# A four-block network on one core: the first attention's probabilities transposed by the DMA engines in its first half

## What is computed

```
x = x + tanh(g_xattn[1]) * _L1_xattn_ref(_layernorm(x), ctx_1024, Wq, Wk, Wv, Wo, gq, gk)

def _L1_xattn_ref(hidden_states, encoder_hidden_states, Wq, Wk, Wv, Wo, gq, gk):
    q = (hidden_states @ Wq).reshape(B, Sq, H, D)            # H = 16 heads, D = 128
    k = (encoder_hidden_states @ Wk).reshape(B, Skv, H, D)
    v = (encoder_hidden_states @ Wv).reshape(B, Skv, H, D)
    q = rmsnorm(q, gq)                    # x * rsqrt(mean(x*x) + 1e-5) * g
    k = rmsnorm(k, gk)
    scores = jnp.einsum('bqhd,bkhd->bhqk', q, k) * (1.0 / np.sqrt(D))
    attn = jax.nn.softmax(scores, axis=-1)
    out = jnp.einsum('bhqk,bkhd->bqhd', attn, v)
    return out.reshape(B, Sq, H * D) @ Wo
```

## Time and profile before

| | |
|---|---|
| median of 3 runs | 1055.88 us (1055.86 to 1058.92) |
| the profiled execution's own time | 1059.89 us |
| its span | 1058.6 us |
| PE busy in the span | 936.7 us, 88% |
| attention1 (first scores to last result) | from 242.7 to 553 us of the span |
| one pass of its first half | 9.15 us |

### The profile page before, as it was taken

One profiled execution on the slowest core, in us unless ns is written; L12 is line 12 of the kernel. 1 busy time (PEld: TensorE's weight loads), 2 busy tenths in 40 slices (PEclk: granted clock), 3 DMA queues, 4 the chain that ended last, 5 costly groups with the idle time before them and its releaser, 6 DMA issues.

```text
span 1058.6 us, 14861 instructions
## 1 busy us (share of the span) xinstructions
PE 936.7 (88%) x4790; PEld 669.3 (63%) x4790; DVE 725.1 (68%) x1877; ACT 520.7 (49%) x1346; POOL 302.5 (29%) x284
## 2 busy tenths in 40 slices
PE   7878789999999999999999989877589988979667
PEld 3323334567999998888977767754355655545455
DVE  5899894245777677678676445576978965576764
ACT  4665672135666666566653434354346552123331
POOL 3767692121111112155101324234232200010210
PEclk8878899999999999999999999999899999989789
DMA  9500001001111164113103446312100003211201
GB/s 363 228 0 0 1 0 50 1 30 45 35 41 46 45 236 153 31 62 94 46 1 119 147 133 191 128 65 60 51 1 1 2 1 141 78 46 31 87 1 41
DMA packets 28500, 75.00 MB, mean 71 GB/s; under 512 B 4092, under 2 KB 5382, under 8 KB 27656
## 3 DMA queue, kind: packets, MB, share of 16 engines
q1 hardware_dynamic: 24344, 63.81, 17.6%
q0 software_dynamic: 3072, 8.39, 2.5%
q10 hardware_dynamic: 1008, 1.86, 0.6%
HBM read 52.03 MB, written 22.02 MB: 70 GB/s over the span
## 4 chain that ended last, share of the span: by engine, by line
PE 62%; DVE 15%; ACT 3%; issue 3%; DMA 1%; SPq 1%; POOL 1%; another core or an unknown queue 0%; DVEq 0%; POOLq 0%; ACTq 0%
PE psum L2195 5%; PE psum L1071 5%; PE psum L1796 5%; PE psum L1277 4%; PE psum L1288 4%; PE psum L927 4%; PE psum L1257 4%; PE psum L1268 2%; PE psum L938 2%; PE psum L1810 2%; PE psum L1095 2%; PE psum L2214 2%; PE psum L2816 2%; PE psum L2458 2%; DVE arena L2492 2%
## 5 line engine op out<-in xcount | busy, mean ns | idle before, releaser
L1167 POOL TENSOR_TENSOR arena<-arena,mhalf 128x8 f32<-128x8 f32 x32 | 53.4, 1670 | 232.6 <-DVE arena L1144 232.6
L1389 DVE SCALAR_TENSOR_TENSOR X<-psum,arena,X 128x256 f32<-128x256 f32 x128 | 56.0, 479 | 64.9 <-PE psum L1288 64.9
L455 POOL TENSOR_TENSOR arena<-arena 128x512 f32<-128x512 f32 x64 | 82.2, 1307 | 8.6 <-PE psum L545 5.1
L855 DVE TENSOR_TENSOR_SCAN arena<-psum,arena 128x512 f32<-128x512 f32 x64 | 74.8, 1210 | 7.9 <-ACT psum L711 6.8
L1331 ACT ACTIVATE arena<-psum,arena 128x256 f32<-128x256 f32 x128 | 59.9, 477 | 35.9 <-DVE arena L1368 33.5
L1796 PE MATMUL psum<-arena 128*128 x248 | 66.6, 391 | 10.6 <-DVE arena L1891 8.8
L2477 ACT ACTIVATE arena<-psum,arena 128x240 f32<-128x240 f32 x128 | 57.4, 463 | 32.3 <-DVE arena L2491 16.4
L545 PE MATMUL psum<-arena,ident 128*128 128x512 f32 x128 | 69.4, 669 | 0.1
L1288 PE MATMUL psum<-arena 128*128 128x256 f32 x256 | 65.9, 380 | 1.2 <-DVE X L1389 1.1
L1257 PE MATMUL psum<-arena 128*128 128x256 f32 x256 | 65.8, 380 | 0.0
L1277 PE MATMUL psum<-arena 128*128 128x256 f32 x256 | 65.8, 380 | 0.0
(11 more groups left out here) (367 smaller groups left out, 2255.7 us busy)
## 6 DMA issues: line engine op xcount, KB each, us to landing
arena<-in_w SPq DMA_DIRECT2D x32, 384.0 KB, 3.1
tokens<-arena SPq DMA_DIRECT2D x2, 4096.0 KB, 22.8
arena<-tokens SPq DMA_DIRECT2D x32, 256.0 KB
results<-arena SPq DMA_DIRECT2D x32, 256.0 KB
arena<-in_moe SPq DMA_DIRECT2D x17, 384.0 KB, 3.1
arena<-in_moe SPq DMA_DIRECT2D x4, 1536.0 KB, 12.8
arena<-in_w SPq DMA_DIRECT2D x2, 1024.0 KB, 6.1
arena<-in_gu SPq DMA_DIRECT2D x1, 1280.0 KB, 7.2
```

The lines of the kernel that those rows point to most:

```text
L455: nc.gpsimd.tensor_tensor(m.HC[:, v, :], m.Hs[:, v, :], m.Cs[:, s % 2, :], ALU.mult).then_inc(*tick("HC", s, c))
L855: nc.vector.tensor_tensor_scan(m.Hs[:, 2 * (s % 2) + c, :], bank[m.bank_dA[c]], input_of(m, s, c), 0.0, ALU.mult, ALU.add).then_inc(*tick( ...
```

## The change

In units 2 to 31 (`BY_DMA`) PE no longer transposes the probabilities and ACT no longer copies them. Instead, POOL copies `Pr` into two planes of 16-bit halves of the float32 words (`halves`, 1024 elements a partition), SP issues one DMA transpose of these 256 KB within the core's SBUF, and POOL puts the planes together again in `PT` (`joined`, 1024 elements). Units 0, 1 and 32 to 63 go the old way.

In all units `attend` and `result` come one unit later (`attend(u-2)`, `result(u-3)`). The queries are no longer multiplied by their root: DVE normalises only the keys, and the queries' root goes into the scale of the exponentials and into `nb`. Queries are turned ahead of the keys, and for passes 1 to 15 into banks 2 and 3. The POOL root of a pass comes a step later, in the even step in which DVE wants it. Weights of passes 5 to 20 are issued by ACT; SP has passes 0 to 4, then the 30 transposes, then the next stages' weights, then passes 21 to 31. In `Pr` the two key halves are now apart.

```diff
+    BY_DMA = range(2, 32)
...
+        k.at = 23856
+        self.halves = [k.place(2, 2 * S, dt=U16)]
+        self.turned = [k.place(2, 2 * S, dt=U16) for _ in range(2)]
...
+        self.halves.append(k.place(2, 2 * S, dt=U16))
...
+def planes(v):
+    return v.bitcast(U16).rearrange("p (n h) -> p h n", h=2)
...
+def attention1_sp(k, m):
+    mamba_left(k, k.sp)
+    a1_weights(k, m, 0, k.sp, k.nc.sync)
+    k.nc.sync.dma_start(m.ctok, k.io["ctok"]).then_inc(*k.s.landed("ctok_in"))
+    for N in range(1, 5):
+        a1_weights(k, m, N, k.sp, k.nc.sync)
+    a1_turned_sp(k, m)
...
+def a1_turned_sp(k, m):
+    for u in m.BY_DMA:
+        k.sp.wait_ge(*k.s.at("a1_H", u))
+        if u - 2 in m.BY_DMA:
+            k.sp.wait_ge(*k.s.at("a1_J", u - 2))
+        k.nc.sync.dma_start_transpose(m.turned[u % 2].rearrange("p h (g i) -> p (h g) i", i=P),
+                                      m.halves[u % 2].rearrange("p h n -> p (h n)")).then_inc(*k.s.landed(f"a1_D{u % 2}", u))
...
+def a1_turn_bank(N, q):
+    return 3 - q if 0 < N < 16 else 7 - q
...
-        k.pe.wait_ge(*k.s.at("a1_N", N))
+        if q:
+            k.pe.wait_ge(*k.s.at("a1_R", N, 1))
+        else:
+            k.pe.wait_ge(*k.s.at("a1_N", N))
...
-    nc.vector.tensor_scalar(m.ss[:, p], m.ss[:, p], 1.0 / m.HD, 1e-5, ALU.mult, ALU.add).then_inc(*tick("a1_var", N))
+    nc.vector.tensor_scalar(m.ss[:, p, 0], m.ss[:, p, 0], 1.0 / m.HD, 1e-5, ALU.mult, ALU.add)
+
+    nc.vector.tensor_scalar(m.ss[:, p, 1], m.ss[:, p, 1], 1e-5 * m.HD, None, ALU.add).then_inc(*tick("a1_var", N))
...
-    k.nc.vector.tensor_tensor(v, v, m.rr[:, N % 3].unsqueeze(3).broadcast_to([P, 2, HT, m.HD]),
+    k.nc.vector.tensor_tensor(v, m.Kr[:, :, N, :] if N < m.NH else v,
+                              m.rr[:, N % 3, 0].unsqueeze(2).broadcast_to([P, HT, m.HD]),
                               ALU.mult).then_inc(*k.s.tick("a1_N", N))
...
+        k.pool.wait_ge(*k.s.at("a1_E", 2 * (N - 3) + 1))
...
-        transposed(u)
+        if u not in m.BY_DMA:
+            transposed(u)
...
-        if u >= 1:
-            attend(u - 1)
+        if u >= 2:
+            attend(u - 2)
...
-        if u >= 2:
-            result(u - 2)
+        if u >= 3:
+            result(u - 3)
...
+                                     scale=m.rr[:, u // 2 % 3, 1, 2 * (u % 2) + j:2 * (u % 2) + j + 1], accum_out=m.rs[:, u % 4, j:j + 1])
...
+        if not first and N < 16:
+            a1_weights(k, m, N + 5, act, nc.scalar)
...
+        dve.wait_ge(*at("a1_rr", u // 2))
+        nc.vector.scalar_tensor_tensor(m.nb[:, w, :], m.mx[:, w, :], -1.0, m.rr[:, u // 2 % 3, 1, 2 * w:2 * w + 2],
+                                       ALU.mult, ALU.mult).then_inc(*tick("a1_nb", u))
...
+    def halves(u):
+        pool.wait_ge(*at("a1_E", u))
+        if u - 2 in m.BY_DMA:
+            pool.wait_ge(*at(f"a1_D{u % 2}", u - 2))
+        nc.gpsimd.tensor_copy(m.halves[u % 2], planes(m.Pr[:, u % 2].rearrange("p c j k -> p (c j k)"))).then_inc(
+            *k.s.tick("a1_H", u))
+
+    def joined(u):
+
+        pool.wait_ge(*at(f"a1_D{u % 2}", u))
+        pool.wait_ge(*at("a1_A", u - 2))
+        nc.gpsimd.tensor_copy(planes(m.PT[:, u % 2].rearrange("p c i -> p (c i)")),
+                              m.turned[u % 2]).then_inc(*k.s.tick("a1_J", u))
...
-        if not first and N + 3 < m.PASSES:
-            a1_root_pool(k, m, N + 3)
+        if u in m.BY_DMA:
+            halves(u)
+        if u - 1 in m.BY_DMA:
+            joined(u - 1)
+        if first and 1 <= N < m.PASSES - 2:
+            a1_root_pool(k, m, N + 2)
```

More of the change, by code:

```diff
@@ L9 @@
 BF16 = mybir.dt.bfloat16
+U16 = mybir.dt.uint16
 ACT = mybir.ActivationFunctionType
@@ L1031, in __init__, with cut, turned_over @@
         self.Kr = k.place(HT, self.NH, HD)
+        k.at = 23856
+        self.halves = [k.place(2, 2 * S, dt=U16)]
+        self.turned = [k.place(2, 2 * S, dt=U16) for _ in range(2)]
+        assert k.at <= FIRST
+        k.at = LAST - 512
+        self.halves.append(k.place(2, 2 * S, dt=U16))
+    def cut(self, u):
+        return ("a1_H" if u in self.BY_DMA else "a1_T", u)
+    def turned_over(self, u):
+        return ("a1_J" if u in self.BY_DMA else "a1_PT", u)
     @staticmethod
@@ L1042, in mamba_left, with a1_landed, a1_weights, attention1_last_sp @@
     eng.wait_ge(*k.s.at("HC", 31, 1))
[L1045 to L1055, removed]
+def planes(v):
+    return v.bitcast(U16).rearrange("p (n h) -> p h n", h=2)
+def a1_landed(N):
+    return f"a1_{'v' if 5 <= N < 21 else 'w'}{N % 2}"
+def a1_weights(k, m, N, eng, queue):
+    if N >= 2:
+        eng.wait_ge(*k.s.at("a1_P", N - 2, 1))
+        if N - 2 < m.NH:
+            eng.wait_ge(*k.s.at("a1_M", N - 2))
+    queue.dma_start(m.W[:, N % 2, :], k.io["w1"][N % m.NH]).then_inc(*k.s.landed(a1_landed(N), N))
+def attention1_sp(k, m):
[5 more added lines that the diff above has]
+    a1_turned_sp(k, m)
+def attention1_last_sp(k, m):
+    for N in range(21, m.PASSES):
+        a1_weights(k, m, N, k.sp, k.nc.sync)
+def a1_turned_sp(k, m):
[5 more added lines that the diff above has]
+                                      m.halves[u % 2].rearrange("p h n -> p (h n)")).then_inc(*k.s.landed(f"a1_D{u % 2}", u))
 def a1_project_pe(k, m, N, q):
@@ L1125, in a1_turned_act @@
 def a1_turned_act(k, m, N):
-    for q in range(2):
+    for q in (1, 0):
         k.act.wait_ge(*k.s.at("a1_turn", N, q))
@@ L1326, in exponentials @@
         if u >= 2:
-            act.wait_ge(*at("a1_T", u - 2))
+            act.wait_ge(*at(*m.cut(u - 2)))
         if u >= 4:
@@ L1330, in exponentials, with turned @@
         for j in range(2):
-            e = nc.scalar.activation(m.Pr[:, w, j, :], bank[w][:, j * S:(j + 1) * S], ACT.Exp,
-                                     bias=m.nb[:, w, j:j + 1], scale=m.SCALE, accum_out=m.rs[:, u % 4, j:j + 1])
+            e = nc.scalar.activation(m.Pr[:, w, :, j, :], bank[w][:, j * S:(j + 1) * S].rearrange("p (c k) -> p c k", c=2),
+                                     ACT.Exp,
+                                     bias=m.nb[:, w, j:j + 1],
+                                     scale=m.rr[:, u // 2 % 3, 1, 2 * (u % 2) + j:2 * (u % 2) + j + 1], accum_out=m.rs[:, u % 4, j:j + 1])
         e.then_inc(*tick("a1_E", u))
+    def turned(u):
+        act.wait_ge(*at("a1_T", u))
+        if u >= 2:
+            act.wait_ge(*at("a1_A", u - 2))
+        nc.scalar.copy(m.PT[:, u % 2, :, :],
+                       bank[2 + u % 2].rearrange("p (t d) -> p t d", t=2)).then_inc(*tick("a1_PT", u))
     exponentials(0)
@@ L1352, in attention1_act @@
             a1_projected_act(k, m, N + 3, 1)
+        if u not in m.BY_DMA:
+            turned(u)
+        if not first and N < 16:
+            a1_weights(k, m, N + 5, act, nc.scalar)
         step(beside[u // 32])
@@ L1403, in attention1_dve @@
         inverse(u)
-        if u >= 1:
-            attended(u - 1)
         if u >= 2:
-            result(u - 2)
+            attended(u - 2)
+        if u >= 3:
+            result(u - 3)
         if first and N + 2 < m.PASSES:
@@ L1412, in attention1_dve @@
         step(beside[u // 32])
+    attended(m.UNITS - 2)
+    result(m.UNITS - 3)
     attended(m.UNITS - 1)
@@ L3732, in sync_program @@
     key_weights_sp(k, st.mamba)
-    attention1_sp(k, st.attention1, range(0, 20))
+    attention1_sp(k, st.attention1)
     dense_left(k, k.sp)
@@ L3736, in sync_program @@
     a2_first_sp(k, st.attention2)
-    attention1_sp(k, st.attention1, range(20, 32))
+    attention1_last_sp(k, st.attention1)
     sorted_sp(k, st.moe1)
```

39 lines of the change are left out of this document (15 added, 24 removed).

## The result

The changed kernel is slower: 1063.97 us (6 runs, 1058.37 to 1066.87) against 1057.4 for the kernel before on the same chips, a ratio of 1.0057, 95% interval [1.0031, 1.0083], or some 6.0 us. The profiled execution of the changed kernel took 1063.15 us with a span of 1061.8.

The account below looks back on a forecast made before the run. PE was taken to bound the first half of attention1, busy throughout each 9.15 us pass. Terms -13.05 - 0.81 + 2.2 - 1.8 + 1.0 = -12.5 us gave a median of 1043.4 us, range 1038 to 1064.

Parts of the forecast that it names:

- rival C: First-half transpose loop or DMA engines cost more than saved, from 5.2 us landing on: 1065 us or more; chance 0.20.
- the side "slower": Chance of the whole kernel being measurably slower than before: 0.23.
- PE loses 13.05 us: First half of attention1: 30 units each lose a 0.435 us group of transposes, so a pass falls to 8.28 us.
- L = 3 to 4 us: Time from issue to landing of a 256 KB DMA transpose in the first half's new loop; it fits up to 4.4.
- line of 60 ns a packet: Upper estimate for the transpose: 256-byte packets at 60 ns, 64 an engine, 3.8 us plus 2 fixed, landing in 5.8.
- These are nothing in the sum: First-half passes: DVE stays under 6.64 and ACT under 6.24 us of 8.28, so their changes cost nothing while PE covers them.
- the second half at -1.8: Four chain pieces of key and query normalisation, halved, are each some 0.5 us shorter: -1.8 us together (0 to -3).
- at the same price: ACT's exponentials with a scale from a column were taken to cost the same as with a constant.
- 1.6 us to spare: First-half even step: POOL's moved root ends at +4.6, DVE needs it at about +6.2 us, so the wait costs nothing.
- Pass 21: +2.2 (0 to 5): Around the first half's end, PE newly waits about 2.2 us for pass 21's weights, queued behind the expert weights.
- Start and drain at +1.0: Start of the stage, with banks 2 and 3 shared, and the longer drain at its end: +1.0 us together.
- 1.04 us as forecast: Each POOL copy of 1024 elements in the first half takes 1.04 us; four and a root make 5.80 of 8.28.

Follow-up runs that it names:

- e6_late: The changed kernel with ACT issuing the weights of passes 5 to 20 later, behind the next even step's turned copies; ratio to before 1.0009.
- e7_best: The changed kernel with keys turned first in the second half, and weights of passes 5 to 22 issued by ACT, later; 1049.01 us, ratio to before 0.9901.
- e1_order: The changed kernel with keys turned ahead of queries again in passes 16 to 31; 1057.87 us, ratio to before 1.0013.
- e2_before_order: The kernel before with only the new turn order, queries ahead of keys in all passes; ratio to before 1.0079.
- e8_scale: The changed kernel with a constant instead of the column of roots as the exponentials' scale; 1059.57 us, one run.
- e3_no_weights: The changed kernel without the weight transfers of passes 5 to 20 and PE's waits for them; ratio to before 0.9984.

## Why the prediction was wrong, step by step

The forecast was 1043.4 us, 12.5 below the kernel before; measured were 6 above. The 1063.97 us lie just inside the upper end of the range, 1064, but that end stood for rival C, a loop that binds on every pass, and this was not what happened; the side "slower" had 0.23.

- **PE loses 13.05 us.** Right in size: with nothing else in the way (e6_late, e7_best) a pass is 8.27 us, 0.88 less than before. The changed kernel kept 7.8 of 11.9 us between turns 3 and 16.
- **L = 3 to 4 us.** Right: 3.1. Rival C's line of 60 ns a packet was wrong: the transposes did go in 256-byte packets, but these are short (below). The slack of the loop over this L is 0.4 to 1.4 us by the prediction's own sum, 8.28 - 3.9 - L.
- **"These are nothing in the sum" (DVE and ACT), and the second half at -1.8.** This is the step that failed. The prediction names that queries are turned ahead of keys nowhere among the costs. It followed the PE list of a first-half pass, where the swap is free, and for the second half it counted only what became shorter. There the swap moved the release of bank 7 behind one more copy, 0.57 us a pass. Turns 20 to 31 took 7.8 us more, 7.5 of which went with the old order (e1_order); the order alone costs 5.5 there (e2_before_order), and 1.7 came with the granted clock in one pass. It is the largest single term of the result. A rival "a bank comes free later" was not on the list. The -1.8 for the halved normalisation did not come either: with the order mended, turns 20 to 31 take 109.4 us against 109.1 before. One of the four pieces of the earlier trace rows shows why. PE stood for 0.66 us behind the exponentials in the kernel before (first line); in e7_best it stands for only 0.30 there, and then 0.50 more for ACT's copy of the turned keys:

```profile
460.94 0.66 PE L1268 MATMUL psum<-ident,arena 128*128 128x128 f32 x4 [0.66 <-ACT arena L1331]
448.16 0.66 PE L1319 MATMUL psum<-ident,arena 128*128 128x128 f32 x4 [0.30 <-ACT arena L1385]
449.31 0.91 PE L1118 MATMUL psum<-arena,cT 128*128 128x128 f32 x6 [0.50 <-ACT arena L1183]
```

  Exponentials "at the same price" were wrong too: 564 ns instead of 477.
- **The weights on ACT's queue.** They were weighed only by what their issue costs ACT. That they share the 16 DMA engines with a transpose whose slack was given as 0.5 to 1.4 us, and can go out in the same moment, was not put together: 4.1 us. DMA share 0.13 was an average. What a late join does was told wrongly as well: not PE at `attend` stood for it, but POOL's root and with it DVE's normalisation. For the root the prediction had 1.6 us to spare and called the wait nothing.
- **Pass 21: +2.2 (0 to 5).** The mechanism was right, the measured wait 2.8 us in the changed kernel and the stretch +3.3. In e1_order, with time won behind the start of the burst and the clock at 0.50, the stretch was +7.
- **Start and drain at +1.0.** The drain alone was +2.3.
- **POOL.** `halves` took 1.04 us as forecast, `joined` 1.34, at times 1.80, not 1.04; DVE rose to 7.66 us in a pass and not below 6.64. Neither bound a pass by itself.

With three more edits (e7_best) the kernel is 10.5 us faster than before, not far from the 12.5 forecast. The terms agree less well than the sums: the first half gives 12.7 us, there is no wait for pass 21, nothing comes from the second half, and the drain costs 2.3. What the change does to PE was costed well; what came with it was costed where it helps and not where it delays.

## What to carry to other kernels

When a change reorders two operations that write different PSUM banks, look in every stage for who takes each bank next; a swap that is free in one half can stall another. A transfer put on another queue is free only if no transfer on a tight loop leaves at the same time: put it beside the one that has slack. What stands behind a long burst on a queue lands when the burst is through, so time won between the start of the burst and the first use turns into waiting; time won ahead of the burst moves both.

## What the runs showed of the hardware

- **DMA transposes within SBUF.** 256 KB landed in 3.0 to 3.1 us when nothing else was under way, 1.23 us of it on SP's issue. One of them fills a stretch of 3.5 us like this (packets, MB, share of 16 engines):

```profile
q1 hardware_dynamic: 1056, 0.26, 39.0%
```

  39% of 3.5 x 16 us over 1056 packets are 21 ns for each 256 bytes, about 1.4 us an engine. So 256 KB pass in 1.4 us, some 190 GB/s. That is half of what the prediction quotes from the Trainium skill, "Advanced Engine Details and Errata", X-Bar Transpose: 350 to 400 GB/s. Nor did its 10.5 us a unit come, worked out from the 1309 ns for one block that the Trainium skill has in "VectorE: DVE Perf Modes", The three transpose paths: one instruction turned all eight blocks in 3.1 us. With the weights issued 0.04 us behind it one took 5.6 us. Some 1.3 us of that are its packets' later start (309.2, above); the rest is open.
- **VectorE and GpSimd can hold each other up.** A 128x4 instruction that takes 0.17 us took 1.31 beside a POOL copy that began 0.06 us earlier:

```profile
301.66 1.34 POOL L1499 COPY arena<-arena 128x1024 uint16<-128x1024 uint16 x1
301.72 1.31 DVE L1196 TENSOR_SCALAR arena<-arena 128x4 f32<-128x4 f32 x1
302.88 0.16 DVE L1198 TENSOR_SCALAR arena<-arena 128x4 f32<-128x4 f32 x1
```

  The Trainium skill has this in "SBUF — State Buffer", Who interferes with whom: the two share a pair of SBUF ports as an exclusive lock, which some VectorE instructions take, `tensor_scalar` in a 2-port mode among them, and whoever issues first keeps the other out for the whole instruction; a VectorE instruction with two SBUF inputs contends with GpSimd's reads. The trace agrees in both directions: POOL's 1.55 us above, beside a two-input multiplication that began 0.03 us earlier, is the other one. In which mode the 128x4 instruction ran the trace does not show.
- **A scale from a column** makes an exponential of 256 columns 564 ns instead of 474 to 477.
- **The granted clock** fell to 0.50 around rests of PE, but the length of the rest does not tell when. In e1_order it was 0.50 from 411.2 to 418.0, around a rest of 4.47 us. It fell also at rests of 1.42 us (e6_late, 0.50 from 409.8 to 413.2) and 2.15 us (e8_scale), and in the changed kernel behind 0.57 and 1.08 us; it stayed at 1.00 behind 2.84 us in the changed kernel, and behind 0.56 and 1.08 us in e3_no_weights.
